# A graph layer and a mixture of eight experts on one core: the first chunk's row numbers found on chip

## The reference

```
# graph layer
h = layernorm(x) @ W.T + b
out[row] += deg[row]**-0.5 * deg[col]**-0.5 * h[col]     # over all edges and self loops
x = x + out
# experts, on flat = layernorm(x)
logits = flat @ router_w.T + router_b
topk_vals, topk_idx = top_k(logits, 2);  topk_w = softmax(topk_vals)
for e in range(8):
    cw = sum(where(topk_idx == e, topk_w, 0))
    y = gelu(flat @ w1[e].T + b1[e]) @ w2[e].T + b2[e]    # 1024 -> 512 -> 1024
    acc = acc + y * cw[:, None]
x = x + layernorm(acc + flat) * ln_w + ln_b
```

## Time and profile before

| what | value |
|---|---|
| median of 3 runs | 625.63 us (621.92 to 626.75) |
| span of the profiled execution | 619.0 us, 12317 instructions |
| own time of the profiled execution | not given beside its span |
| PE busy | 533.6 us (86%) |
| DVE busy | 470.0 us (76%) |
| ACT busy | 242.4 us (39%) |
| POOL busy | 193.9 us (31%) |
| the chain that ended last | PE 77%, DVE 14% |

### The profile page before, as it was taken

One profiled execution on the slowest core, in us unless ns is written; L12 is line 12 of the kernel. 1 busy time (PEld: TensorE's weight loads), 2 busy tenths in 40 slices (PEclk: granted clock), 3 DMA queues, 4 the chain that ended last, 5 costly groups with the idle time before them and its releaser, 6 DMA issues.

```text
span 619.0 us, 12317 instructions
## 1 busy us (share of the span) xinstructions
PE 533.6 (86%) x3660; PEld 298.1 (48%) x3661; DVE 470.0 (76%) x1295; ACT 242.4 (39%) x358; POOL 193.9 (31%) x199
## 2 busy tenths in 40 slices
PE   1688999899999999995779999999999999999100
PEld 1244554445444555554564655556565656564000
DVE  8879869997174889898858778695868685755397
ACT  5333444324280243435534344343444443401470
POOL 3013000000001165656544535344452543151240
PEclk9999999999899999998699999999999999999655
DMA  6894320333327243445486969798897889173978
GB/s 234 326 380 139 58 46 10 72 77 60 57 95 279 103 158 141 167 138 201 127 303 168 271 211 233 251 231 254 219 263 200 260 222 284 28 166 77 263 209 279
DMA packets 59565, 112.34 MB, mean 181 GB/s; under 512 B 33490, under 2 KB 33903, under 8 KB 59504
## 3 DMA queue, kind: packets, MB, share of 16 engines
q1 hardware_dynamic: 49424, 80.02, 37.7%
q0 software_dynamic: 8896, 27.38, 21.3%
q10 hardware_dynamic: 1184, 4.20, 2.0%
HBM read 71.75 MB, written 33.67 MB: 170 GB/s over the span
## 4 chain that ended last, share of the span: by engine, by line
PE 77%; DVE 14%; issue 3%; DMA 2%; ACT 2%; DVEq 1%; POOL 0%; ACTq 0%; POOLq 0%; SPq 0%
PE ps L1794 7%; PE ps L1795 7%; PE ps L1913 7%; PE ps L1914 6%; PE ps L1915 6%; PE ps L1892 5%; PE ps L1893 5%; PE ps L1894 5%; PE ps L1703 4%; PE ps L1642 4%; PE ps L1705 4%; PE ps L1704 4%; PE ps L1874 4%; DVE wbufs L1279 2%; PE ps L1623 2%
## 5 line engine op out<-in xcount | busy, mean ns | idle before, releaser
L613 POOL DMA_INDIRECT acc_rows<-work,ids_out x24 | 53.0, 2208 | 106.1 <-DVE work L1497 106.1
L1794 PE MATMUL ps<-wbufs,rows_and_counts 128*128 128x512 f16 x200 | 75.8, 379 | 0.5 <-DVE wbufs L1279 0.5
L1892 PE MATMUL ps<-rows_and_counts,wbufs 128*128 128x336 f16 (+2 forms) x256 | 74.9, 298 | 1.4 <-DVE rows_and_counts L1437 0.8
L1795 PE MATMUL ps<-wbufs,rows_and_counts 128*128 128x512 f16 x200 | 75.8, 379 | 0.0
L1893 PE MATMUL ps<-rows_and_counts,wbufs 128*128 128x336 f16 (+2 forms) x256 | 74.9, 298 | 1.0 <-issue 1.0
L1894 PE MATMUL ps<-rows_and_counts,wbufs 128*128 128x336 f16 (+2 forms) x256 | 74.9, 298 | 0.0
L1913 PE MATMUL ps<-wbufs,rows_and_counts 128*128 (+1 forms) x192 | 72.9, 379 | 1.6 <-issue 1.3
L1452 DVE SCALAR_TENSOR_TENSOR wbufs<-stage,wbufs 128x1024 f16<-128x1024 f32 x56 | 67.2, 1218 | 8.4 <-ACT wbufs L927 8.3
L1914 PE MATMUL ps<-wbufs,rows_and_counts 128*128 (+1 forms) x192 | 72.8, 379 | 0.0
L1915 PE MATMUL ps<-wbufs,rows_and_counts 128*128 (+1 forms) x192 | 72.8, 379 | 0.0
L526 POOL TENSOR_TENSOR work<-work 128x1024 f16<-128x1024 f32 x9 | 19.2, 2130 | 168.9 <-ACT work L900 168.9
(11 more groups left out here) (308 smaller groups left out, 1054.1 us busy)
## 6 DMA issues: line engine op xcount, KB each, us to landing
stage<-wst_in SPq DMA_DIRECT2D x72, 512.0 KB
...
```

The lines of the kernel that those rows point to most:

```text
L1794: mm(o, ct_hi[:, cs], hs[:, at:at + HALF], start=(m == 0), stop=False, skip_group_check=True)
L1795: mm(o, ct_hi[:, cs], hs[:, D + at:D + at + HALF], start=False, stop=False, skip_group_check=True)
L1892: mm(o, wbufs[:, ds(w + ws, P)], x_hi, start=(j == 0), stop=False)
```

## The change

The first chunk's row numbers are no longer read back from the table. In `place(r)` DVE compares the numbers 0 to 383 (`slot_no16`) with each row's slot for expert 0, times 1 if the row chose expert 0 (`slot_hot`, a matrix of 0 and 1). PE multiplies it with the column of row numbers (`number(r)`), so that each slot receives the number of its row; DVE sums over the tiles and writes whole numbers (`ids_known`). `number(r-3)` stands in PE's loop behind `aggregate(r, 0)`. `place(6)` is moved ahead, into `add_agg(8)`. POOL gathers the first two tiles of chunk 0 after `xs_lo` of tile 8.

The first rows' high and low halves are turned apart as float16 (`turn_first`, no sum in PSUM), one ACT copy takes both (`turn_copied`), and DVE's subtraction L1365 goes. Their up products (`up_first`) stand amid the last routings, as a list written by hand. The GELU and the halves of the first 256 columns are made apart from those of the third tile. Pieces 14 and 15 of the weights are split later, and pieces 18 and 19 loaded later.

```diff
-        zeros16 = early[:, at:at + P // 2].bitcast(F16)
+        zeros16 = sb("zeros16", [P, P], F16)
...
+            g.iota(slot_no16, [[1, CH]], base=0, channel_multiplier=0, allow_small_or_imprecise_dtypes=True
+                   ).then_inc(numbers_done, 1)
...
-                    if r - 2 == FIRST_TILES:
-
-                        pool.wait_ge(agg_done, 2 * NT)
+                    if r - 1 == FIRST_TILES:
+
                         pool.wait_ge(x2_first_stored, 16 * FIRST_TILES)
-                        pool.wait_ge(ids_in, 16)
+                        pool.wait_ge(first_ids_done, 1)
                         for i in FIRST:
-                            gather_first(i, ids_first, FIRST_TILES)
+                            gather_first(i, ids_known, FIRST_TILES)
+                    if r == NT + 1:
+
+                        pool.wait_ge(x2_stored, 16 * NT + 16 * (NT - FIRST_TILES))
+                        pool.wait_ge(third_id_done, 1)
+                        for i in range(len(FIRST), CT):
+                            gather_first(i, ids_known, NT)
...
-                if 2 <= r < NT:
+                if 2 <= r < NT - 2:
                     split_lo(PIECES + r - 2, e_hi[0], e_lo[0])
+            for q in range(2 * PIECES - 2, 2 * PIECES):
+                split_lo(q, e_hi[0], e_lo[0])
...
-                if r == FIRST_TILES + 1:
-                    sp.wait_ge(scattered_first, 16 * 2 * FIRST_TILES)
-                    sp.dma_start(ids_first[:], slot_table_v[:, 0, 0:len(FIRST)]).then_inc(ids_in, 16)
-                if 2 <= r:
+                if 2 <= r < NT - 2:
                     piece(PIECES + STAGES + r - 2, True)
+            for q in range(2 * PIECES + 2, 2 * PIECES + STAGES):
+                piece(q, True)
             sp.wait_ge(cw_done, 1)
...
+            def turn_copied(j):
+                act.wait_ge(first_done, j + 1)
+                a.activation(x4[:, j * 2 * CH:(j + 1) * 2 * CH].rearrange("p (h c) -> p h c", h=2)[:, :, 0:FIRST_CH],
+                             first_ps[j % 2].rearrange("p (h c) -> p h c", h=2), ACT.Copy).then_inc(first_turned, 1)
...
+                if r == NT:
+                    act.wait_ge(agg_done, 2 * NT)
+                    turn_copied(0)
+                    turn_copied(1)
...
-            for j in range(2, DK):
-                first_turned(j)
-                if j - 2 < EARLY:
-                    piece_hi(0, j - 2, e_hi[1])
+            for j in range(4, DK):
+                turn_copied(j)
+            split_hi(2 * PIECES - 1, e_hi[0])
+            for j in range(EARLY // 2):
+                piece_hi(0, j, e_hi[1])
+            act.wait_ge(first_up_done, 1)
+            for f in range(FK):
+                a.activation(y32[:, f * CH:f * CH + FIRST_CH], first_up_ps[f], ACT.Gelu, bias=b1t[:, f:f + 1],
+                             scale=1.0 / WSCALE).then_inc(first_gelu_done, 1)
...
             for j in range(DK):
                 turned(0, j, FIRST_CH)
+            for j in range(EARLY // 2, EARLY):
+                piece_hi(0, j, e_hi[1])
...
+                if r == FIRST_TILES + 1:
+                    place(FIRST_TILES - 1)
                 dve.wait_ge(std_done, len(NORM_GROUPS) + r + 1)
...
             def place(r):
                 dve.wait_ge(rank_done, r + 1)
+                st3.did(v.tensor_tensor(chosen[:], choice(r)[:, 0:1], choice(r)[:, NE:NE + 1], ALU.add))
                 st3.link(v.tensor_tensor(slot_of[:], rank_ps[:, 0:NE], carry[:], ALU.add))
+                if r >= 2:
+                    dve.wait_ge(slot_hot_used, r - 1)
+                first = 0 if r < FIRST_TILES else FIRST_CH
+                v.tensor_scalar(slot_hot[r % 2][:, first:], slot_no16[:, first:], slot_of[:, 0:1], chosen[:],
+                                ALU.is_equal, ALU.mult).then_inc(slot_hot_done, 1)
...
+                if r == FIRST_TILES + 2:
+                    dve.wait_ge(slot_hot_used, FIRST_TILES)
+                    st3.link(v.tensor_reduce(ids_sum[:, 0:len(FIRST)], ids_ps[:, 0:len(FIRST), 0:FIRST_TILES], AXX, ALU.add))
+                    v.tensor_copy(ids_known[:, 0:len(FIRST)], ids_sum[:, 0:len(FIRST)]).then_inc(first_ids_done, 1)
                 if 2 <= r:
                     choose(r - 2)
...
-            for j in range(DK - EARLY, DK):
-                first_turned(j)
-                if j >= DK - EARLY:
-                    piece_lo(0, j - (DK - EARLY), (e_hi[1], e_lo[1]))
+            for j in range(EARLY // 2):
+                piece_lo(0, j, (e_hi[1], e_lo[1]))
...
+            for f in range(FK):
+                dve.wait_ge(first_gelu_done, f + 1)
+                halves_of(slice(f * CH, f * CH + FIRST_CH))
             for j in range(DK):
                 turned(0, j, FIRST_CH)
+            for j in range(EARLY // 2, EARLY):
+                piece_lo(0, j, (e_hi[1], e_lo[1]))
...
+            def number(r):
+                pe.wait_ge(slot_hot_done, r + 1)
+                for i in range(CT) if r < FIRST_TILES else range(len(FIRST), CT):
+                    ins = mm(ids_ps[:, i, r:r + 1], slot_hot[r % 2][:, i * P:(i + 1) * P], token16[:, r:r + 1],
+                             start=True, stop=True)
+                ins.then_inc(slot_hot_used, 1)
...
-            for r in range(NT + 2):
-                if r < NT:
-                    aggregate(r, 0)
+            for r in range(NT):
+                aggregate(r, 0)
+                if r >= 3:
+                    number(r - 3)
+                if r == FIRST_TILES + 2:
+                    pe.wait_ge(first_ids_done, 1)
                 if r >= 2:
                     route(r - 2)
...
+            route(NT - 2)
+            turn_first(0)
+            turn_first(1)
+            turn2(NT - 1)
+            up_first(0)
+            turn_first(2)
+            rank(NT - 2)
+            number(NT - 3)
+            up_first(1)
+            turn_first(3)
+            route(NT - 1)
+            up_first(2)
+            rank(NT - 1)
+            number(NT - 2)
+            number(NT - 1)
+            up_first(3)
+            turn_first(4)
+            for j in range(4, DK):
+                if j + 1 < DK:
+                    turn_first(j + 1)
+                up_first(j)
```

157 lines of the change are left out of this document (89 added, 68 removed).

## The result

The changed kernel takes 643.96 us, median of 4 runs (641.19 to 646.65); the kernel before, on the same chip, 623.77 (620.64 to 626.75). The ratio is 1.0323, with a 95% interval of 1.0276 to 1.0369: slower by 20 us. 636.4 was forecast, within 623.5 to 640.5. The direction held; the size did not.

What follows compares the result with a forecast made beforehand. PE was taken as the bound, gapless in stage 3. Terms 4.8 + 2.5 + 3.5 = 10.8 us on the 619.0 span gave 629.8; with 6.6 around it, 636.4 us, range 623.5 to 640.5.

Steps and rivals of the forecast that it cites:

- The signs that were named beforehand: Six L1885 waits of some 0.7, L1863 wait of 2.4, PE pause over 8 us, clock fall, L1493/L540, reading about 48.7.
- Stage 3, iterations 3 to 8: PE's `number(r-3)` waits for DVE's 0/1 matrix: 0.8 us in each of six iterations, 4.8 us later.
- DVE's own growth "hides": In stage 3, DVE's period grows by 0.4 us and has 0.54 idle, so it costs nothing.
- Iteration 9: PE waits 2.4 us for `first_ids_done` in stage 3; with three products 2.5 us later, bounds 2.0 to 3.0.
- The turn: From the last aggregate to DVE's first reading of down: 48.7 us instead of 45.2, 3.5 later; bounds -9.3 to +6.
- The other chain: Table read-back and gathers into chunk 0: weights land at 48.7 us, DVE needs them at 48.5; hides by nothing.
- The rest "shifts as a whole": From chunk 0 on: same instructions and PE bound, so it only starts later.
- The sum: 4.8 + 2.5 + 3.5 = 10.8 us on the profiled span of 619.0, giving 629.8.
- The first rival: Third turning starts under 28 us after the last aggregate; turn gains 9.3 instead of losing 3.5: 623.6 us; chance 0.17.

Runs made afterwards that it cites:

- n1: Changed kernel with `number` of iterations 3 to 8 moved behind `rank(r-2)`; 644.57 us, ratio 1.036 to the kernel before.
- n2: Changed kernel with the first two tiles' ids reduced inside `place(6)` and `number(6)` put inside `aggregate(9, 0)`; 639.52 us, ratio 1.0241 to the kernel before.
- p2: Changed kernel with 32 increments of an unused semaphore early on ACT, shifting only its instruction stream; 640.06 us, ratio 1.027 to the kernel before.
- p5: Kernel before the change, with 64 one-column products added ahead of PE's first turning; 619.78 us, ratio 0.9957 to the kernel before.
- n3: Changed kernel with ACT and DVE turning the third tile first, plans and all four weight pieces behind it; 649.47 us, ratio 1.0438 to the kernel before.
- p1: Changed kernel with 64 one-column products ahead of PE's first turning, shifting only PE's stream; 641.96 us, ratio 1.0304 to the kernel before.

## Why the prediction was wrong

The signs that were named beforehand came, all but DVE's first reading at 48.7: the six waits, the one at L1863, PE's pause of 8.65 with the clock falling in it, L1493 beside L540. The mechanism of the loss was right. Its size was not, 20.5 us of span for 10.8, by terms that were mis-sized or put at nothing.

- **Stage 3, iterations 3 to 8** (4.8 us). Right in mechanism: six waits at L1885, 0.65 each as idle, 0.91 by the step of the iterations, so 5.5. The comparison of 384 columns took 0.38 (L1381), where 0.30 was taken from the row of 320 columns. The sentence that DVE's own growth "hides" was true only as long as PE waited for the matrix: n1 shows DVE's period at 10.88, so even without the wait about 0.5 would have stayed in each late iteration. The sum of DVE's growth, 0.4, left out that a small instruction could come to stand beside POOL's `xs_lo` for longer than before: 1.97 at L1396, where before it was a cast at 1.21.
- **Iteration 9** (2.5 us). The wait came as worked out, 2.29 for 2.4. The failed step is that its price was taken as its length. The granted clock was at half behind it, from about 288.8 to 292.2, and cost 1.7 more. The earlier trace rows had shown a fall after a pause; I used that for the turn and not for this wait. n2 took out both, 3.9.
- **The turn** (+3.5 us; measured 8.0). In the prediction's count, from the end of the last aggregate, 294.11, the steps up to the third tile held: first up products at 27.3 (26.2), DVE's turning at 35.8 (35.1), pieces held beside POOL's L540 as I had let them be, 3.32 for two, and PE idle for 8.65 with the clock falling. What failed is the step from there to the first reading, 13.6 in the sum and 17.4 measured. ACT stood 3.34 us without a releaser; with ACT's stream shifted (p2) it takes 13.1, and the reading comes at 48.5 in this count, against 48.7 forecast. That this lands on the forecast is in part luck. The kernel before has such a stop of ACT as well, at 316.74 (DVE's 1.22 in the earlier trace rows comes behind it), so the 45.2 that the forecast is set against holds one, of some 1.9 us; in p5, without it, the turn is 43.7 in place of 45.5. By the executions of p2 and p5 the turn became 5.0 us longer, and not 3.5; the other 3 us of the measured 8.0 are the difference of two layouts. The prediction had no term for that.
- **The other chain** ("it hides by nothing"). In the same count the weights' gather was done at 45.8, before the reading at 53.2, so it did hide. n3 shows how close it stands: a gather held for 4.5 us cost the turn more than turning the third tile early had won.
- **The rest "shifts as a whole".** From chunk 1 on it does: 256.0 and 256.3. Between the two chunks' first readings it did not, +2.0, and p1, where the stop of 3.03 is gone and the column 32.8, shows that it is PE's stop.
- **The sum.** Forecast 10.8, measured 20.5. The difference of 9.7 is 0.7 for the waits' size, 1.7 for the clock and 0.1 around them, 4.5 in the turn, 2.0 in front of chunk 1, 0.3 in the rest and 0.4 ahead of stage 3, where nothing was changed. The first rival (third tile not held) was tried by n3, and its own condition, a turning before 28 or so, brought no gain, since the table chain took over; n3 also moved all four weight pieces behind that turning, so it is no clean test of the turning alone.
